# Two products of gate weights beside each of 26 maxima in the lead-in of the attention

## The chip, the cores and the metric

The kernel runs on one core of a Trainium2 chip. The metric is device time in microseconds (us), less is better. The engines are TensorE (PE; its weight loads are PEld), VectorE (DVE), ScalarE (ACT), GpSimd (POOL) and SyncE (SP, which here issues the DMAs). TensorE runs at one of two granted clocks, 2.4 GHz (shown as 1.00) or 1.2 GHz (0.50).

## The reference, cut to what matters

The reference is a macaron block on x of shape (2, 1024, 256): a feed-forward part, causal attention, the feed-forward part again.

```python
x = x + 0.5 * ffn(layernorm(x), w_gate, w_up, w_down)      # silu(gate) * up, 2 of 4 kept, down
x = x + attn(layernorm(x), Wq, bq, Wk, bk, Wv, bv, Wo, bo) # 32 heads of 8, 8 key/value heads, rotary, causal
x = x + 0.5 * ffn(layernorm(x), w_gate, w_up, w_down)
```

Inside the attention: `scores = q k^T / sqrt(8)`, masked above the diagonal, then `softmax(scores) @ v`, then `@ Wo + bo`. The softmax subtracts each row's maximum, and this kernel computes that maximum from the scores themselves.

## The kernel before, in words

The program of each engine is written out by hand and the phases follow one another: feed-forward 1, the projections to q, k and v (`qkv`), attention, feed-forward 2. An engine does its instructions in the order in which they stand; between engines there are semaphores.

The attention goes over 16 groups (2 batches by 8 key/value heads; 4 query heads each). In a group TensorE does three kinds of products:

- **maxima** (`maximum_scores`, written to `att_m_ps`, four banks of PSUM): 48 per group, each 128 queries by up to 512 keys, with the operands' 64 rows in the upper half of the array (`m_lane`, partitions 64 to 127). DVE takes the row maximum of each (L1418 where the causal mask is added, L1421 elsewhere), which frees the bank.
- **scores** (`s_head`, written to `att_s_ps`, three banks): keys by queries, with the operands in the lower half of the array (`s_lane`, partitions 0 to 63). ACT takes the exponential (L1471).
- **values** (`value_unit`, `att_o_ps`, L1370): the exponentials times v, over all 128 rows.

A **turn** (`turn_shift`, L1333) transposes the joined maxima of half a group, so that they can be loaded by DMA as two further rows of q and be subtracted in the scores' product.

The order within a group is the string `ORDER`. Ahead of group 0 there is a **lead-in**, the loop over `first_steps` in `tensor`: maxima 0 to 63 (48 of group 0 and 16 of group 1) with the two turns of group 0 among them, and the first 12 scores. Maxima 0 to 3 stand still earlier, in the projections (`first_scores`). Up to maximum 37 there are only maxima and one turn (it stands ahead of maximum 26); from maximum 38 (`S_FROM`) every second maximum is followed by a score. `banks_free(pe, "s")` waits until DVE has read the last unit of the projections (L817) out of the banks that the scores will use. `wait_bank` lets maximum n wait until DVE has taken the maximum four before it.

`wg[0]` is the high part of the feed-forward's gate weights, in SBUF since feed-forward 1.

Of the kernel before, what the change touches and what calls it, by code (L numbers as in the profile page):

```python
# [1161 lines left out]
        dve.tensor_tensor(rows, self.y_ps[pair % 2][:].rearrange("p t c -> p (t c)"), rows, ALU.add).then_inc(self.y_added, 1)  # L1162


def attention_programs(nc, ctx, group_rows, v, region, s_ps, m_ps, o_ps, output, normed, ident_bf, x, bo_row, T, HD, earlier):

# [4 lines left out]
    q, k, m_loaded = group_rows.q, group_rows.k, group_rows.m_loaded  # L1173
    s_lane, m_lane = group_rows.s_lane, group_rows.m_lane
# [43 lines left out]
    S_BANKS = 3  # L1218
# [14 lines left out]
    def steps(g):  # L1233

        count = dict.fromkeys("smtv", 0)
        for kind in ORDER:
            n = count[kind]
            count[kind] += 1
            if kind == "s":
                n += (g * SU + AHEAD) * QPK  # L1240
                taken = not FIRST_HEADS <= n < GROUPS * SU * QPK
            elif kind == "m":
                n += (g + 1) * MU + FIRST_MAXIMA
                taken = n >= GROUPS * MU
            elif kind == "t":
                n += (g + 1) * QC
                taken = n >= GROUPS * QC
            else:
                n += g * SU
                taken = n < LEAD_IN  # L1250
            if not taken:
                yield kind, n
# [7 lines left out]
    def sb(name, shape, dt):  # L1260
        return region.take(f"att_{name}", shape, dt)
# [14 lines left out]
    bo = sb("bo", [P, x.shape[2]], F32)  # L1276
# [25 lines left out]
    banks_free, v_ready = earlier  # L1302
    WEIGHTS_AT = 2
    FIRST_SCORES = M_BANKS
    S_FROM = 38
    STAGE_AT = LEAD_IN
    assert FIRST_HEADS <= (MU - S_FROM + 1) // 2 + FIRST_TURNS[1]
    PAIR_AFTER = {1: 0, 2: 1, 5: 2, 6: 3}
# [5 lines left out]
    def wait_bank(pe, step):  # L1314
        if step in BANK_USER:
            kind, n = BANK_USER[step]
            pe.wait_ge(m_taken if kind == "m" else shift_t_ready, n + 1)

    def maximum_scores(pe, n):
        g, m = divmod(n, MU)  # L1320
        t, h, kc, cols = M_UNITS[m]
        if m == 0:
            pe.wait_ge(m_loaded[g % 2], 16 * 2 * (g // 2 + 1))
        wait_bank(pe, ("m", n))
        pe.matmul(m_ps[BANK["m", n]][:, :cols], q[g % 2][m_lane, h, t * P:(t + 1) * P],  # L1325
                      k[g % 2][m_lane, kc * N:kc * N + cols],
                  start=True, stop=True).then_inc(m_done, 1)

    def turn_shift(pe, n):
        pe.wait_ge(shift_ready, n + 1)  # L1330
        wait_bank(pe, ("t", n))
        for t in range(TPC):
            last = pe.transpose(t_ps[BANK["t", n]][:, t * P:(t + 1) * P],  # L1333
                                shift[n % QC][:, t, :, :].rearrange("p h s -> p (h s)"), ident_bf[:])
        last.then_inc(t_done, 1)
# [7 lines left out]
    def tensor(pe):  # L1343
        def s_head(n):
            g, u, h = n // (SU * QPK), n // QPK % SU, n % QPK
            qc, pieces = S_UNITS[u]
            if h == 0 and u == 0:
                pe.wait_ge(s_loaded[g % 2], 16 * 2 * (g // 2 + 1))
            if h == 0 and u in CHUNK_FIRST:
                pe.wait_ge(shift_loaded[qc], 16 * QPK * (g + 1))  # L1350
            if n >= S_BANKS:
                pe.wait_ge(exp_done, n - S_BANKS + 1)
            for kb, q0, w, at in pieces:
                last = pe.matmul(s_ps[n % S_BANKS][:, at:at + w], k[g % 2][s_lane, kb * P:(kb + 1) * P],  # L1354
                                 q[g % 2][s_lane, h, qc * N + q0:qc * N + q0 + w], start=True, stop=True)
            last.then_inc(s_done, 1)

        def value_unit(g, u):
            qc, pieces = S_UNITS[u]
            n = g * SU + u  # L1360
            if u == 0:
                pe.wait_ge(v_staged, g + 1)
            if u in CHUNK_FIRST:
                pe.wait_ge(o_taken, QC * g + qc)
            pe.wait_ge(exp_done, QPK * (n + 1))
            if u in DIAGONAL:
                pe.wait_ge(masked, g * sum(map(len, MASKS)) + sum(map(len, MASKS[:u + 1])))
            for kb, q0, w, at in pieces:
                for h in range(QPK):
                    last = pe.matmul(o_ps[32 * h:32 * (h + 1), q0:q0 + w], vs[g % 2][:, kb, :],  # L1370
                                     probs[u % len(probs)][:, h, at:at + w],
                                     start=(u in CHUNK_FIRST), stop=(u in CHUNK_LAST), skip_group_check=True)
            last.then_inc(pv_done, 1)

        def group(g):
            for kind, n in steps(g):
                if kind == "s":
                    s_head(n)
                elif kind == "m":
                    maximum_scores(pe, n)  # L1380
                elif kind == "t":
                    turn_shift(pe, n)
                else:
                    u = n % SU
                    value_unit(g, u)
                    if g == LAST and u in PAIR_AFTER:
                        if PAIR_AFTER[u] == 0:
                            pe.wait_ge(m_taken, GROUPS * MU)
                            pe.wait_ge(shift_t_ready, GROUPS * QC)
                        output.project(pe, PAIR_AFTER[u])  # L1390
                    if g == LAST and u == TURN_AFTER:
                        normed.transpose(pe, 0)

        pe.sem_inc(pv_done, len(probs))
        heads = 0
        for kind, n in first_steps[FIRST_SCORES:]:
            if kind == "t":
                turn_shift(pe, n)
                continue
            maximum_scores(pe, n)  # L1400
            if n >= MU or (n >= S_FROM and (n - S_FROM) % 2 == 0):
                if heads == 0:
                    banks_free(pe, "s")
                if heads < FIRST_HEADS:
                    s_head(heads)
                    heads += 1
        for u in range(LEAD_IN):
            value_unit(0, u)
        for g in range(GROUPS):
            group(g)  # L1410
# [94 lines left out]
    def gpsimd(pool):  # L1505
# [19 lines left out]
        def split_maxima(g, qc):  # L1525

            if qc:
                pool.wait_ge(top_ready, g + 1)
                whole = top[:]
            else:  # L1530
                pool.wait_ge(m_taken, g * MU + MU_HALF)
                whole = maxima[:, :, :TPC, 0].rearrange("p h t -> p t h")
            pool.tensor_copy(shift[qc][:, :, :, 0], whole).then_inc(high_ready, 1)
            pool.wait_ge(high_ready, QC * g + qc + 1)
            pool.tensor_tensor(shift[qc][:, :, :, 1], whole, shift[qc][:, :, :, 0], ALU.subtract)\
                .then_inc(shift_ready, 1)
# [15 lines left out]
        def group(g):  # L1552
            for kind, n in steps(g):
# [4 lines left out]
                elif kind == "m" and n % MU == MU - 1:  # L1558
                    split_maxima(n // MU, 1)
                elif kind == "v" and n % SU == STAGE_AT and g < LAST:  # L1560
                    pool.wait_ge(pv_done, g * SU + len(probs))
# [106 lines left out]
def build(nc, x_in, w_qkv, bias_cols, bv, w_o, bo, w_gate, w_up, w_down, cos_t, sin_t, out, HD=8, SPLIT=4):  # L1668
    B, T, C = x_in.shape
# [6 lines left out]
    with ExitStack() as ctx:  # L1676
# [3 lines left out]
        x = sb("x", [P, TILES, C], F32)  # L1680
        ident = sb("ident", [P, P], F32)
        ident_bf = sb("ident_bf", [P, P], BF16)
        parts = ("hi", "lo")
        wg = [sb(f"wg_{n}", [P, KT, BLKS, J, P], F32R) for n in parts]
# [15 lines left out]
        v = low.take("v", [P, KVH, TILES, HD], F32)  # L1700
        group_rows = GroupRows(nc, ctx, low, q_rows, k_rows, T, HD)
# [30 lines left out]
        for b in range(BLKS):  # L1732
# [11 lines left out]
        qkv, follower, earlier = qkv_programs(nc, ctx, x, normed1, TILES // FIRST, qkv_raw[:], qkv_raw_loaded, bias_cols, bv, cos_t, sin_t,  # L1744
                                              q_rows, k_rows, v, group_rows, qkv_homes, qk_ps, between)
# [7 lines left out]
        normed2 = NormedChunks(nc, ctx, "ffn2", x, ident, N, xt_ps=xt2,  # L1753
                               region=Homes(hole, {"ffn2_xn": m_hole, "ffn2_xt_hi": m_hole, "ffn2_xt_lo": m_hole}))
        late_hole = Region(nc, hole.at)
        att_region = Region(nc, above)
        late = Region(nc, late_at)
        output = Output(nc, ctx, late, hole, x, w_o.rearrange("(k p) n -> p k n", p=P), inverse_rows, KVH, C // HD // KVH, HD, T, N, out_ps)
        attention, before_groups, first_scores, first_maxima, hooks = attention_programs(
            nc, ctx, group_rows, v, att_region, s_ps, m_ps, o_ps, output, normed2, ident_bf, x, bo, T, HD, earlier)  # L1760
        between["fills"] += [lambda pool: group_rows.fill_q(pool, 0),
                    lambda pool: (group_rows.fill_k(pool, 0), before_groups(pool)),
                    lambda pool: (group_rows.fill_q(pool, 1), group_rows.fill_k(pool, 1))]
# [53 lines left out]
```

## Time and profile before

| | us |
|---|---|
| median of 3 runs | 829.38 (826.87 to 832.43) |
| the profiled execution, its own time | 832.21 |
| its span, first to last instruction | 830.7 |
| PE busy | 774.4 (93%) |
| DVE busy | 721.2 (87%) |
| ACT busy | 491.5 (59%) |
| attention's 512 maxima of L1418, on DVE | 234.3 |
| attention's 256 maxima of L1421, on DVE | 175.9 |
| mean granted clock of TensorE | 0.965 |

A row of the timeline is: start, duration, engine, line, operation, what is written and read, the array's rows by columns, the shape, and in brackets how long the engine was idle before it and what ended that. Matmuls are pipelined, so the distance between two starts is what one costs in a series, and not its duration.

### The profile page before, as it was taken

To read this page: it belongs to the slowest core of one execution; us is meant where nothing else is said; L and a number is where in the kernel's file an instruction comes from. 1 tells how busy PE (TensorE), PEld (TensorE's weight loads), DVE (VectorE), ACT (ScalarE), POOL (GpSimd) and SP (SyncE) were. 2 spreads that over 40 slices of the span, in tenths; PEclk is the share of its full clock that TensorE was granted. 3 is DMA by queue.
4 is the path that set the end of the run, shared out by engine and by line. 5 is a ranking of instruction groups with operands and counts; after the bars stand their busy time and mean duration, and the time that the engine had idled before them with its cause. 6 is when DMAs were issued, how large, how long until landed. Compare 5 with 4: busy or idle time off the path is not lost.

```text
span 830.7 us, 15658 instructions
## 1 busy us (share of the span) xinstructions
PE 774.4 (93%) x5168; PEld 508.7 (61%) x5168; DVE 721.2 (87%) x1862; ACT 491.5 (59%) x949; POOL 262.3 (32%) x359
## 2 busy tenths in 40 slices
PE   4999999989899999999999989999899999999996
PEld 3787887977654544444444444444444468888886
DVE  3989999986797999999999989999987259999997
ACT  6444443311135888888888868888678734443441
POOL 1143533058720332322322222155315210534330
PEclk9999999999857999999999989999999999999999
DMA  8100000026913321233311332533313000000001
GB/s 294 53 0 2 0 1 1 1 107 173 297 33 69 71 66 37 61 74 72 70 41 39 72 70 54 132 67 76 72 21 85 15 8 1 1 26 1 26 2 51
DMA packets 21968, 48.62 MB, mean 59 GB/s; under 512 B 3744, under 2 KB 8224, under 8 KB 21376
## 3 DMA queue, kind: packets, MB, share of 16 engines
q1 hardware_dynamic: 21824, 47.56, 21.9%
q8 instruction: 41, 0.67, 0.4%
q14 instruction: 39, 0.32, 0.1%
q10 hardware_dynamic: 64, 0.07, 0.0%
HBM read 19.63 MB, written 14.16 MB: 41 GB/s over the span
## 4 chain that ended last, share of the span: by engine, by line
PE 61%; DVE 20%; issue 8%; POOL 5%; ACT 5%; DMA 1%; PEldq 0%; DVEq 0%; PEld 0%; SPq 0%; ACTq 0%; POOLq 0%
PE att_o_ps L1370 17%; PE att_m_ps L1325 15%; PE att_s_ps L1354 10%; PE ffn_gate L218 5%; PE ffn_up L218 5%; PE ffn_y_ps L351 5%; DVE ffn_hs L524 2%; DVE ffn_h L566 2%; POOL qkv_turned L859 2%; POOL qkv_parts L864 2%; ACT att_probs L1471 2%; DVE att_maxima L1421 2%; DVE att_scratch L1418 1%; DVE ffn_rank L510 1%; DVE ffn_pair_max L498 1%
## 5 line engine op out<-in xcount | busy, mean ns | idle before, releaser
L1471 ACT ACTIVATE att_probs<-att_s_ps 128x512 f32<-128x512 f32 (+1 forms) x640 | 314.3, 558 | 92.4 <-PE att_s_ps L1354 90.4
L1325 PE MATMUL att_m_ps<-k,q 64*128 64x512 f32 (+3 forms) x768 | 240.9, 413 | 15.5 <-DVE att_maxima L1418 13.6
L1418 DVE CUSTOM_DVE_ANT_0 att_scratch<-att_m_ps,att_causal 128x512 bf16<-128x512 f32 (+3 forms) x512 | 234.3, 485 | 20.9 <-PE att_m_ps L1325 17.9
L1354 PE MATMUL att_s_ps<-q,k 64*128 64x512 f32 (+3 forms) x768 | 223.3, 392 | 3.9 <-ACT att_probs L1471 3.9
L1325 PEld LDWEIGHTS att_m_ps<-k,q 64*128 64x128 f32 x768 | 132.9, 196 | 105.2 <-DVE att_maxima L1418 57.4
L1421 DVE TENSOR_REDUCE att_maxima<-att_m_ps 128x1 f32<-128x512 f32 x256 | 175.9, 687 | 11.5 <-PE att_m_ps L1325 11.3
L1370 PE MATMUL att_o_ps<-att_probs,att_vs 128*32 128x512 f32 (+3 forms) x1536 | 161.4, 508 | 1.6 <-POOL att_probs L1510 1.6
L1510 POOL TENSOR_SCALAR_AFFINE_SELECT att_probs<-att_probs 128x512 f32<-128x512 f32 x128 | 79.9, 637 | 262.3 <-ACT att_probs L1471 262.3
L1354 PEld LDWEIGHTS att_s_ps<-q,k 64*128 64x128 f32 x768 | 122.5, 190 | 64.8 <-ACT att_probs L1471 62.0
L630 POOL TENSOR_TENSOR ffn_hs_lo<-ffn_hs,ffn_hs_hi 128x512 fp32r<-128x512 f32 x48 | 76.6, 1621 | 106.4 <-ACT ffn_hs_hi L427 106.4
L454 ACT ACTIVATE ffn_a<-ffn_h 128x512 f32<-128x512 f32 x64 | 40.5, 633 | 106.8 <-DVE ffn_h L566 106.8
L351 PE MATMUL ffn_y_ps<-wd_hi,ffn_hs_hi 128*128 128x256 f32 x256 | 73.8, 288 | 6.2 <-DVE x L554 2.7
L351 PE MATMUL ffn_y_ps<-wd_lo,ffn_hs_hi 128*128 128x256 f32 x256 | 73.0, 285 | 0.0
L351 PE MATMUL ffn_y_ps<-wd_hi,ffn_hs_lo 128*128 128x256 f32 x256 | 72.9, 285 | 0.0
L1370 PEld LDWEIGHTS att_o_ps<-att_probs,att_vs 128*32 128x32 f32 x1536 | 34.1, 110 | 56.4 <-issue 41.8
L566 DVE TENSOR_TENSOR ffn_h<-ffn_up,ffn_silu 128x512 f32<-128x512 f32 x64 | 43.6, 682 | 23.0 <-ACT ffn_silu L449 22.0
L218 PE MATMUL ffn_gate<-ffn_xt_hi,wg_hi 128*128 128x512 f32 x128 | 52.2, 408 | 3.6 <-DVE ffn_h L566 1.6
L351 PEld LDWEIGHTS ffn_y_ps<-wd_hi,ffn_hs_hi 128*128 128x128 f32 x256 | 49.4, 193 | 9.4 <-DVE x L554 2.9
L218 PE MATMUL ffn_gate<-ffn_xt_lo,wg_hi 128*128 128x512 f32 x128 | 50.8, 397 | 0.9 <-DVE ffn_xt_lo L199 0.9
L427 ACT ACTIVATE ffn_hs_hi<-ffn_hs 128x512 fp32r<-128x512 f32 x56 | 35.0, 632 | 27.0 <-DVE ffn_hs L524 27.0
L218 PE MATMUL ffn_gate<-ffn_xt_hi,wg_lo 128*128 128x512 f32 x128 | 50.9, 398 | 0.0
L218 PE MATMUL ffn_up<-ffn_xt_lo,wu_hi 128*128 128x512 f32 x128 | 50.7, 396 | 0.0
(114 smaller groups left out, 1166.8 us busy)
## 6 DMA issues: line engine op xcount, KB each, us to landing
q_rows<-qkv_parts SPq DMA_DIRECT2D x16, 512.0 KB, 4.6
q<-q_rows SPq DMA_DIRECT2D x16, 512.0 KB, 4.6
q<-q SPq DMA_DIRECT2D x16, 512.0 KB, 4.3
k_rows<-qkv_parts SPq DMA_DIRECT2D x8, 256.0 KB, 3.0
k<-k_rows SPq DMA_DIRECT2D x16, 128.0 KB, 5.2
k<-k SPq DMA_DIRECT2D x16, 128.0 KB, 4.3
q<-att_shift_t SPq DMA_DIRECT2D x128, 4.0 KB
out_num<-att_sums SPq DMA_DIRECT2D x128, 16.0 KB
```

Of the source, the lines that this page charges most:

```text
L218: last = pe.matmul(bank, w[w_part], xt[:, k, :], start=(k == 0 and n == 0), stop=(k == self.KT - 1 and n == 2))
L351: last = pe.matmul(y_ps[:, t, :], hp[:, blk, j, rows], wp[:, blk, j, :], start=(blk == 0 and j == 0 and m == 0 and t % 2 == 0), stop=(blk ...
L454: act.activation(a[:, blk, j, :], h[:, blk, j, :], ACT.Abs).then_inc(abs_ready, 1)
L566: dve.tensor_tensor(h[:, blk, j, :], gu[j % 2][1][:], silu[:, j % 2, :], ALU.mult).then_inc(h_ready, 1)
L630: pool.tensor_tensor(hs_lo[:, blk, j, :], hs[:, j, :], hs_hi[:, blk, j, :].bitcast(F32), ALU.subtract).then_inc(lo_ready, 1)
L1325: pe.matmul(m_ps[BANK["m", n]][:, :cols], q[g % 2][m_lane, h, t * P:(t + 1) * P], k[g % 2][m_lane, kc * N:kc * N + cols], start=True, stop ...
L1354: last = pe.matmul(s_ps[n % S_BANKS][:, at:at + w], k[g % 2][s_lane, kb * P:(kb + 1) * P], q[g % 2][s_lane, h, qc * N + q0:qc * N + q0 + w ...
L1370: last = pe.matmul(o_ps[32 * h:32 * (h + 1), q0:q0 + w], vs[g % 2][:, kb, :], probs[u % len(probs)][:, h, at:at + w], start=(u in CHUNK_FI ...
L1418: dve.tensor_tensor_reduce(out=scratch[bank][:, :n], in0=m_ps[bank][:, :n], in1=causal[:, N - n:], scale=1.0, scalar=LOWEST, op0=ALU.add, ...
L1421: dve.tensor_reduce(top_of, m_ps[bank][:, :n], mybir.AxisListType.X, ALU.max).then_inc(m_taken, 1)
L1471: act.activation(probs[u % len(probs)][:, h, SPAN[u]], s_ps[n % S_BANKS][:, SPAN[u]], ACT.Exp, scale=SCALE).then_inc(exp_done, 1)
L1510: pool.affine_select(out=blk, in_=blk, compare_op=ALU.is_ge, fill=0.0, base=0, pattern=[[0, QPK], [1, P]], channel_multiplier=-1).then_inc ...
```

## The change

After each of the maxima 12 to 37, TensorE does two further products (`HOLD = 2`) of 64 rows by 128 columns with 512 moving columns, both operands out of `wg[0]`, with the operands in the lower half of the array. They are written to the three banks `att_s_ps`, which nothing reads until the first score overwrites them. The wait for these banks, which stood ahead of the first score (after maximum 38), stands now also ahead of the first added product. No semaphore is raised by the added products and no other engine's program changes.

```diff
-def attention_programs(nc, ctx, ..., T, HD, earlier):
+def attention_programs(nc, ctx, ..., T, HD, earlier, weights):
...
     S_FROM = 38
+    HOLD_FROM = 12
+    HOLD = 2
...
             maximum_scores(pe, n)
+            if HOLD_FROM <= n < S_FROM:
+
+                if n == HOLD_FROM:
+                    banks_free(pe, "s")
+                for i in range(HOLD):
+                    pe.matmul(s_ps[(HOLD * n + i) % S_BANKS][:], weights[s_lane, 0, 0, i, :],
+                              weights[s_lane, 0, 0].rearrange("p j q -> p (j q)"), start=True, stop=True)
             if n >= MU or (n >= S_FROM and (n - S_FROM) % 2 == 0):
...
-            nc, ctx, group_rows, v, att_region, s_ps, m_ps, o_ps, output, normed2, ident_bf, x, bo, T, HD, earlier)
+            nc, ctx, group_rows, v, att_region, s_ps, m_ps, o_ps, output, normed2, ident_bf, x, bo, T, HD, earlier, wg[0])
```

On TensorE, where maximum 12 stands (the third row from the top; `att_m_ps` are the maxima, `wg_hi` the added products), before:

```order
L1325 MATMUL att_m_ps<-k_52,q_51 128x384 [waits att_m_taken]
L1325 MATMUL att_m_ps<-k_52,q_51 128x256 [waits att_m_taken]
L1325 MATMUL att_m_ps<-k_52,q_51 128x384 [waits att_m_taken]
L1325 MATMUL att_m_ps<-k_52,q_51 128x256 [waits att_m_taken]
L1325 MATMUL att_m_ps<-k_52,q_51 128x384 [waits att_m_taken]
L1325 MATMUL att_m_ps<-k_52,q_51 128x256 [waits att_m_taken]
L1325 MATMUL att_m_ps<-k_52,q_51 128x512 [waits att_m_taken]
```

and now:

```order
L1327 MATMUL att_m_ps<-k_52,q_51 128x384 [waits att_m_taken]
L1327 MATMUL att_m_ps<-k_52,q_51 128x256 [waits att_m_taken]
L1327 MATMUL att_m_ps<-k_52,q_51 128x384 [waits att_m_taken]
L1408 MATMUL att_s_ps<-wg_hi 128x512 [waits qkv_by_ready]
L1408 MATMUL att_s_ps<-wg_hi 128x512
L1327 MATMUL att_m_ps<-k_52,q_51 128x256 [waits att_m_taken]
L1408 MATMUL att_s_ps<-wg_hi 128x512 x2
L1327 MATMUL att_m_ps<-k_52,q_51 128x384 [waits att_m_taken]
L1408 MATMUL att_s_ps<-wg_hi 128x512 x2
```

Two products stand between each maximum and the next; the maxima keep their own waits and their order.

On TensorE, at the end of the stretch (maximum 37, then 38 and the first scores), before:

```order
L1325 MATMUL att_m_ps<-k_52,q_51 128x384 [waits att_m_taken]
L1325 MATMUL att_m_ps<-k_52,q_51 128x512 [waits att_m_taken]
L1354 MATMUL att_s_ps<-q_51,k_52 128x512 [waits att_shift_loaded0,s_loaded0,qkv_by_ready]
L1325 MATMUL att_m_ps<-k_52,q_51 128x384 [waits att_m_taken]
L1325 MATMUL att_m_ps<-k_52,q_51 128x512 [waits att_m_taken]
L1354 MATMUL att_s_ps<-q_51,k_52 128x512
```

and now:

```order
L1327 MATMUL att_m_ps<-k_52,q_51 128x384 [waits att_m_taken]
L1408 MATMUL att_s_ps<-wg_hi 128x512 x2
L1327 MATMUL att_m_ps<-k_52,q_51 128x512 [waits att_m_taken]
L1356 MATMUL att_s_ps<-q_51,k_52 128x512 [waits att_shift_loaded0,s_loaded0,qkv_by_ready]
L1327 MATMUL att_m_ps<-k_52,q_51 128x384 [waits att_m_taken]
L1327 MATMUL att_m_ps<-k_52,q_51 128x512 [waits att_m_taken]
L1356 MATMUL att_s_ps<-q_51,k_52 128x512
```

From maximum 38 on nothing is added and nothing has moved.

## Rows read from the trace of the kernel before

**Rows 1.** The page: share of the chain that ended last.

```profile
PE 61%; DVE 20%; issue 8%; POOL 5%; ACT 5%; DMA 1%; PEldq 0%; DVEq 0%; PEld 0%; SPq 0%; ACTq 0%; POOLq 0%
```

**Rows 2.** Busy time by stretch: stretch, its length, engines' busy us (instructions), PEclk, DMA share, GB/s.

```profile
220.50:223.90 3.40, 1.80 (x8) 1.05 (x6) 3.40 (x15) 0.63 (x1) 2.60 (x3) 1.00 0.96 278
...
224.00:236.00 12.00, 11.49 (x29) 6.81 (x28) 11.17 (x41) 1.22 (x2) 4.95 (x11) 0.50 0.61 192
236.00:246.00 10.00, 9.85 (x35) 5.89 (x34) 9.96 (x30) 6.20 (x12) 1.60 (x4) 0.50 0.00 1
246.00:258.00 12.00, 11.85 (x52) 6.01 (x50) 8.71 (x38) 3.80 (x8) 2.53 (x6) 0.50 0.47 105
258.00:261.40 3.40, 3.40 (x18) 1.82 (x20) 3.05 (x10) 2.53 (x5) 0.00 (x0) 0.50 0.15 30
261.60:280.00 18.40, 17.65 (x152) 8.65 (x145) 16.46 (x56) 14.83 (x32) 3.53 (x8) 1.00 0.07 17
```

**Rows 3.** DVE in the lead-in: last read of the projections, maxima 8, 12, 16, 32 and 38.

```profile
220.51 0.74 DVE L817 SCALAR_TENSOR_TENSOR qkv_by_sin<-qkv_swapped,qkv_biases,qkv_sin 128x512 f32<-128x512 f32 x1
...
222.81 0.55 DVE L1418 CUSTOM_DVE_ANT_0 att_scratch<-att_m_ps,att_causal 128x384 bf16<-128x384 f32 x1
...
224.45 0.55 DVE L1418 CUSTOM_DVE_ANT_0 att_scratch<-att_m_ps,att_causal 128x384 bf16<-128x384 f32 x1
...
226.37 0.69 DVE L1421 TENSOR_REDUCE att_maxima<-att_m_ps 128x1 f32<-128x512 f32 x1 [0.19 <-issue]
226.98 0.28 DVE L1418 CUSTOM_DVE_ANT_0 att_scratch<-att_m_ps,att_causal 128x128 bf16<-128x128 f32 x1
...
231.41 0.69 DVE L1421 TENSOR_REDUCE att_maxima<-att_m_ps 128x1 f32<-128x512 f32 x1 [0.64 <-PE att_m_ps L1325]
...
234.24 0.69 DVE L1421 TENSOR_REDUCE att_maxima<-att_m_ps 128x1 f32<-128x512 f32 x1
...
237.46 0.69 DVE L1421 TENSOR_REDUCE att_maxima<-att_m_ps 128x1 f32<-128x512 f32 x1
```

**Rows 4.** Busy time by stretch, where the clock fell.

```profile
223.00:224.00 1.00, 0.91 (x4) 0.53 (x3) 1.00 (x5) 0.63 (x1) 0.26 (x2) 0.94 1.04 401
```

**Rows 5.** PE at the full clock, both halves of the array in series.

```profile
268.44 0.50 PE L1354 MATMUL att_s_ps<-q,k 64*128 64x512 f32 x1
268.78 0.39 PE L1325 MATMUL att_m_ps<-k,q 64*128 64x512 f32 x1
268.78 0.39 PE L1354 MATMUL att_s_ps<-q,k 64*128 64x512 f32 x1
269.01 0.39 PE L1325 MATMUL att_m_ps<-k,q 64*128 64x512 f32 x1
```

**Rows 6.** PE at the low clock, products of one half in series.

```profile
604.19 0.62 PE L1354 MATMUL att_s_ps<-q,k 64*128 64x512 f32 x1
604.51 0.62 PE L1325 MATMUL att_m_ps<-k,q 64*128 64x512 f32 x1
604.61 0.62 PE L1354 MATMUL att_s_ps<-q,k 64*128 64x512 f32 x1
```

**Rows 7.** Busy time by stretch: three later low stretches and what stood before them.

```profile
483.80:486.60 2.80, 1.78 (x13) 1.12 (x17) 2.80 (x10) 2.35 (x7) 0.99 (x3) 1.00 0.88 227
486.90:490.00 3.10, 3.10 (x20) 1.34 (x16) 2.78 (x8) 1.55 (x4) 0.74 (x2) 0.50 0.49 104
490.20:493.40 3.20, 2.31 (x18) 1.28 (x16) 2.61 (x8) 2.02 (x4) 1.16 (x3) 1.00 0.59 123
...
599.40:606.00 6.60, 5.86 (x32) 3.15 (x32) 5.00 (x16) 2.92 (x7) 0.00 (x0) 0.50 0.31 66
```

**Rows 8.** DVE: the maxima of groups 0, 1, 2 and 3 are joined.

```profile
243.49 0.19 DVE L1436 TENSOR_REDUCE att_top<-att_maxima 128x16 f32<-128x32 f32 x1
...
272.30 0.19 DVE L1436 TENSOR_REDUCE att_top<-att_maxima 128x16 f32<-128x32 f32 x1
...
297.79 0.19 DVE L1436 TENSOR_REDUCE att_top<-att_maxima 128x16 f32<-128x32 f32 x1
...
323.29 0.19 DVE L1436 TENSOR_REDUCE att_top<-att_maxima 128x16 f32<-128x32 f32 x1
```

**Rows 9.** The page: weight loads of the scores.

```profile
L1354 PEld LDWEIGHTS att_s_ps<-q,k 64*128 64x128 f32 x768 | 122.5, 190 | 64.8 <-ACT att_probs L1471 62.0
```

More of the change, by code:

```diff
@@ L1162, in add, with attention_programs @@
         dve.tensor_tensor(rows, self.y_ps[pair % 2][:].rearrange("p t c -> p (t c)"), rows, ALU.add).then_inc(self.y_added, 1)
-def attention_programs(nc, ctx, group_rows, v, region, s_ps, m_ps, o_ps, output, normed, ident_bf, x, bo_row, T, HD, earlier):
+def attention_programs(nc, ctx, group_rows, v, region, s_ps, m_ps, o_ps, output, normed, ident_bf, x, bo_row, T, HD, earlier, weights):
     q, k, m_loaded = group_rows.q, group_rows.k, group_rows.m_loaded
```

## The prediction

> **What bounds the kernel now.** I read the page's chain first. TensorE holds 61% of it and DVE 20% [rows 1], so over the whole kernel TensorE's time counts most. That share says little of the 15 us which the change touches, so I next read busy time by stretch around the lead-in [rows 2]. The reader is to see two things there. First, the granted clock is 1.00 up to 223.9, 0.50 from 224 to 261.4, and 1.00 again from 261.6. Second, from 224 to 236, where there are only maxima and one turn, DVE is busy 11.17 of 12 us, and from 236 to 246 it is busy 9.96 of 10. So DVE is the bound up to 246, low clock or not. Between 246 and 258 DVE has only 8.71 busy of 12, and PE 11.85: there the low clock costs something.
>
> Then I read DVE itself [rows 3]. It takes maximum 12 at 224.45 and maximum 38 at 237.46: 26 maxima in 13.0 us, 0.50 each. It waits noticeably for TensorE only once, 0.64 us ahead of maximum 26, behind the turn. Taken singly, a pair of 512 and 128 columns (maxima 16 to 23) costs 0.61 + 0.20 = 0.81 us (226.37 to 226.98, and 0.28 less its overlap).
>
> What the low clock costs as a whole is read from the joins of the maxima [rows 8]: from group 1's to group 2's it is 297.79 - 272.30 = 25.5 us, and the same from 2 to 3; from group 0's to group 1's it is 28.8. So 3.3 us are lost between 243.5 and 272.3, and that is nearly all behind the place of the added products.
>
> **The change, part by part.** It adds 52 products with their 52 weight loads, on TensorE alone, and moves one wait forward. It removes nothing.
>
> *The wait for the banks.* It now stands ahead of the first added product, behind maximum 12. It ends when DVE has done its last read of the projections, at 220.51 + 0.74 = 221.25. Maximum 12 itself needs DVE to be done with maximum 8, which ends at 222.81 + 0.55 = 223.36 [rows 3]. The wait is over 2.1 us before anyone reaches it: 0 us. If that cover were gone, every later maximum would stand behind it; 2.1 us is a lot of cover.
>
> *Does the clock fall all the same?* The mean 0.94 over 223 to 224 puts the fall at 223.88 [rows 4]. The first added product can't start before 223.4. In the 3.4 us before the fall PE is busy 1.80 us and stands idle the rest, since DVE is the slower one [rows 2], and the change can fill at most the last 0.5 us of that. So what the clock was lowered for is still there, and I expect it to fall at about the same place. An execution in which it falls a little later, or not at all, is possible, since the filled stretch begins right there.
>
> *An added product at either clock.* At the full clock two products of 512 columns on one half of the array start 0.23 us apart, while the other half does the same [rows 5]; at the low clock 0.42 us [rows 6]. Two per maximum make 0.47 and 0.85 us (I take 0.425 for one). The maximum itself runs on the other half meanwhile, as s and m do at 268.78, so it adds nothing. But TensorE works in order: maximum n+1 stands behind two products of maximum n, so the pace of the maxima cannot be better than this.
>
> *At the full clock* 0.47 stands against DVE's 0.405 for maxima 16 to 23 and 0.50 on average: TensorE falls back by 8 x 0.065 = 0.5 us and gets it back in the wider maxima behind. DVE's 0.64 us of waiting behind the turn is what can be had back in the best case, but that turn waits for POOL too. Sum about 0 (0.5 either way).
>
> *At the low clock* 0.85 stands against 0.50 (0.41 for maxima 12 to 23). TensorE becomes the bound, and DVE, banks and all, waits for it. Each maximum that falls into a low stretch costs 0.44 us among the first twelve and 0.35 on average. Nothing covers this: the scores from maximum 38 on, the first exponentials and the second turn all stand behind it in order, and DVE takes group 1's maxima as they come.
>
> *How long would it stay low?* That is the price that rows of before can only bound. One end: it comes back after one of the short low stretches seen later, 3.1 us (486.9 to 490.0) to 6.6 us (599.4 to 606.0), in which both halves of the array were kept at work [rows 7]. The other end: it stays low for all 26, as it did from 224 to 261 with PE busy 9.85 of 10 us in one part [rows 2]; a busy TensorE alone does not bring it back. With the added products one half works all the time and the other some third of it, which lies between these cases. I take the longer of the short stretches, 6.6 us, as the nearest row: 6.6 / 0.85 = 8 maxima, 8 x 0.44 = 3.5 us. Of this 0.5 us is cover (maximum 12's scores were ready, at 223.4 + 0.5, before DVE came at 224.45), and the 0.64 us at the turn is no longer waited for separately: 3.5 - 0.5 - 0.6 = **+2.4 us**.
>
> *What comes back.* The 3.3 us lost behind 243.5 would come back only if the clock were high from 246 to 261. The added products end at maximum 37. Behind them come the same maxima and scores as before, paced by DVE, and at the full clock they leave PE idle much as from 490.2 to 493.4, busy 2.31 of 3.2, where the clock fell again [rows 7]. So even a clock held through the 26 maxima falls in 236 to 246, and the costly part behind is as it was: 0 us.
>
> The sum against the profiled execution is 832.2 + 2.4 = 834.6. That execution is 2.8 us above the median of the runs (829.4), so against the median it is 829.4 + 2.4 = **832** (rounded).
>
> **Rule against row.** Three products of a half start 0.34 and 0.23 us apart, each with its own weight load, whose mean is 190 ns [rows 5, 9]; the load is hidden. The Trainium skill ("TensorE: Matmul & The Clock Gate", section "Part 3: Packing small matmuls — row/col tiling") says that a weight load overlaps running matmuls only where the row groups differ, and both added products use the same. By that rule the sum would be that of the fourth rival below; the trace disagrees with it for products in series.
>
> **The rivals.**
>
> *1. The low clock stays (slower).* The same mechanism, its long end: from two thirds of the 26 maxima on. All of them: 26 x 0.85 = 22.1 us for what takes 13.0, so +9.1 us, 838.5; two thirds (17 of them, 12 at 0.44 and 5 at 0.35, less 1.1) +5.9, 835.3. Against it: rows 7, where the clock came back in 3 to 7 us. For it: rows 2, where it didn't in 34 us with PE just as busy. It is over 1% (8.3 us) only if the clock is not back before about the 24th of the 26.
>
> *2. The clock does not fall before the products begin, and they hold it.* Cost about 0, no gain behind either: 829.4. For it: they start within half a microsecond of the fall. Against it: the idle stretch in front is not changed.
>
> *3. It does what it seems to be for (faster).* The clock is high through the lead-in and also behind, to 261. The 3.3 us of the joins and up to 0.9 us of DVE's waits come back: 829.4 - 3.3 = 826.1, at best 825.2. Against it: the ten microseconds without added products.
>
> *4. Every product pays its weight load.* 0.23 + 0.19 = 0.42 us at the full clock too, so 0.85 per maximum for all 26: +9, 838.5. Rows 5 speak against it.
>
> **How the numbers follow.** Chances: the forecast (clock falls, back within the first dozen or so; +1 to +4) 0.38; rival 1 0.28, of which 0.10 for over 1%; rival 2 0.17; rival 3 0.13; rival 4 0.04, of which 0.02 for over 1%. A change of under 1% (8.3 us) can't be told from none by this measurement, the runs before alone spread over 5.6 us. Slower by over 1% has 0.10 + 0.02 = 0.12; faster by over 1% needs twice what rival 3 gives, 0.02; within 1% the rest, 0.86. The range: from 826, which leaves out the better half of rival 3 (0.07), to 837, which takes in rival 1 up to +7.6 and leaves out its end and rival 4 (0.13).
>
> **What would show it.** In the profile after: the clock falls near 224 with the first added products in front of it, and is 0.50 for some 3 to 10 us. In the low part maxima of L1327 start 0.85 us apart and DVE is idle ahead of each, waiting for PE; in the high part 0.47 to 0.6. DVE's join of group 0 moves from 243.5 to about 246. From about 240 to 262 the clock is 0.50 again and the distance of the joins of groups 0 and 1 stays near 28.8. What would make it wrong: a join of group 0 at 243 to 244 (rival 2), 249 to 253 (rival 1 or 4, told apart by the clock), or a distance of 25.5 between the joins (rival 3).

## The result and the profile after

The changed kernel is slower by 0.7%: 837.5 us median (830.2 to 843.3, 20 runs) against 830.4 (826.3 to 840.0, 20 runs) for the kernel before, ratio 1.0073, 95% interval 1.0052 to 1.0094. The ratio leaves out executions over 1.5% above the fastest of their kernel, the medians do not; by the ratio it is 6.1 us, by the medians 7.1. Two later comparisons gave 1.0077 (1.0051 to 1.0104) and 1.0094 (1.0065 to 1.0123). That is within the 1% which I had called no change, but clear of noise. I had forecast +2.4 us.

The profiled execution took 833.9 us (span 832.4), 1.7 more than the profiled one before, and the page looks alike:

```profile
PE 63%; DVE 20%; issue 7%; ACT 5%; POOL 4%; DMA 1%; PEldq 0%; DVEq 0%; PEld 0%; SPq 0%; ACTq 0%; POOLq 0%
...
L1430 DVE TENSOR_REDUCE att_maxima<-att_m_ps 128x1 f32<-128x512 f32 x256 | 175.9, 687 | 11.0 <-PE att_m_ps L1327 10.9
```

Busy time by stretch (length; PE, PEld, DVE, ACT, POOL busy us; PEclk; DMA share; GB/s), to be read against [rows 2]:

```profile
221.50:224.80 3.30, 1.70 (x10) 1.09 (x9) 3.30 (x15) 0.63 (x1) 2.53 (x3) 1.00 1.02 282
225.00:228.00 3.00, 3.00 (x14) 2.54 (x12) 2.28 (x12) 0.63 (x1) 2.28 (x2) 0.50 1.05 400
228.50:240.00 11.50, 11.34 (x72) 8.73 (x70) 10.86 (x34) 1.67 (x2) 2.17 (x9) 1.00 0.30 76
...
242.00:246.00 4.00, 3.98 (x12) 2.12 (x13) 3.96 (x11) 1.75 (x5) 0.15 (x1) 0.50 0.00 0
246.00:258.50 12.50, 12.22 (x53) 6.76 (x53) 9.82 (x42) 4.16 (x8) 3.98 (x10) 0.50 0.36 87
```

The clock still falls, right behind the half-empty stretch (PE busy 1.70 of 3.3 us), with the first added products at 224.4. Here it is back by 228.5. From 242 on it is low again, up to 265.8. On DVE the low part looks like this:

```profile
227.13 0.42 DVE L1427 CUSTOM_DVE_ANT_0 att_scratch<-att_m_ps,att_causal 128x256 bf16<-128x256 f32 x1 [0.29 <-PE att_m_ps L1327]
...
228.31 0.69 DVE L1430 TENSOR_REDUCE att_maxima<-att_m_ps 128x1 f32<-128x512 f32 x1 [0.74 <-PE att_m_ps L1327]
```

DVE now waits for TensorE ahead of maxima 15 and 16; in the kernel before it did so, up to maximum 38, only at the turn [rows 3]. At the turn it still waits, 0.61 us. And TensorE itself, first at the low and then at the full clock:

```profile
226.31 1.05 PE L1408 MATMUL att_s_ps<-wg_hi 64*128 64x512 f32 x2
226.74 0.47 PE L1327 MATMUL att_m_ps<-k,q 64*128 64x128 f32 x1
227.16 1.05 PE L1408 MATMUL att_s_ps<-wg_hi 64*128 64x512 f32 x2
...
229.51 0.61 PE L1408 MATMUL att_s_ps<-wg_hi 64*128 64x512 f32 x2
229.90 0.50 PE L1327 MATMUL att_m_ps<-k,q 64*128 64x512 f32 x1
229.97 0.61 PE L1408 MATMUL att_s_ps<-wg_hi 64*128 64x512 f32 x2
```

A pair of added products starts every 0.85 us (227.16 - 226.31) and then every 0.46 (229.97 - 229.51). The joins, to be read against [rows 8]:

```profile
245.60 0.19 DVE L1445 TENSOR_REDUCE att_top<-att_maxima 128x16 f32<-128x32 f32 x1
...
275.04 0.19 DVE L1445 TENSOR_REDUCE att_top<-att_maxima 128x16 f32<-128x32 f32 x1
...
300.53 0.19 DVE L1445 TENSOR_REDUCE att_top<-att_maxima 128x16 f32<-128x32 f32 x1
```

Executions reach the lead-in at slightly different times. To compare traces I measure from DVE's last read of the projections (L817), which starts at 220.51 in the kernel before and at 221.48 here. From there to group 0's join it is 22.98 us before and 24.12 here, +1.1.

What this one trace does not show is the median's 7 us. Each run lists its mean granted clock, and the time goes with it: of the changed kernel's runs those at 0.977 to 0.979 took 830 to 834 us, those at 0.971 to 0.973 took 835 to 837, those at 0.963 took 841 to 843. But at the same mean clock of 0.967 the kernel before takes 830 to 834 us and the changed one 837 to 840. So the mean clock alone does not explain the 7 us: either the low clock costs more in the changed kernel, because of where it falls, or the added products cost their time whatever the clock is.

### The profile page after: what moved, and what is told of

It reads as the page before. It is cut to its first block, busy times and chain, and to the rows that moved or that the text cites. A ratio compares the mean times of both kernels' runs of the same rounds, so it can differ in the third digit from the quotient of the medians.

```text
span 832.4 us, 15762 instructions
## 1 busy us (share of the span) xinstructions
PE 772.8 (93%) x5220; PEld 512.3 (62%) x5220; DVE 724.5 (87%) x1862; ACT 492.0 (59%) x949; POOL 262.2 (32%) x359
## 4 chain that ended last, share of the span: by engine, by line
PE 63%; DVE 20%; issue 7%; ACT 5%; POOL 4%; DMA 1%; PEldq 0%; DVEq 0%; PEld 0%; SPq 0%; ACTq 0%; POOLq 0%
PE att_o_ps L1372 17%; PE att_m_ps L1327 15%; PE att_s_ps L1356 10%; PE ffn_gate L218 6%; PE ffn_up L218 5%; PE ffn_y_ps L351 4%; DVE ffn_hs L524 3%; DVE ffn_h L566 2%; ACT att_probs L1480 2%; DVE att_scratch L1427 1%; PE out_y_ps L1152 1%; DVE att_maxima L1430 1%; DVE ffn_pair_min L499 1%; POOL qkv_turned L859 1%; PE att_s_ps L1408 1%
## 5 line engine op out<-in xcount | busy, mean ns | idle before, releaser
L1327 PE MATMUL att_m_ps<-k,q 64*128 64x512 f32 (+3 forms) x768 | 237.6, 405 | 15.4 <-DVE att_maxima L1427 12.8
L1356 PE MATMUL att_s_ps<-q,k 64*128 64x512 f32 (+3 forms) x768 | 220.6, 389 | 4.2 <-ACT att_probs L1480 4.0
L1327 PEld LDWEIGHTS att_m_ps<-k,q 64*128 64x128 f32 x768 | 129.8, 191 | 101.3 <-DVE att_maxima L1427 58.4
L351 PEld LDWEIGHTS ffn_y_ps<-wd_hi,ffn_hs_hi 128*128 128x128 f32 x256 | 49.4, 193 | 10.2 <-DVE x L554 2.9
L351 PEld LDWEIGHTS ffn_y_ps<-wd_lo,ffn_hs_hi 128*128 128x128 f32 x256 | 49.6, 194 | 1.5
L218 PE MATMUL ffn_up<-ffn_xt_hi,wu_hi 128*128 128x512 f32 x128 | 50.5, 394 | 0.0
```

What stands on the lines that cost most here:

```text
L218: last = pe.matmul(bank, w[w_part], xt[:, k, :], start=(k == 0 and n == 0), stop=(k == self.KT - 1 and n == 2))
L351: last = pe.matmul(y_ps[:, t, :], hp[:, blk, j, rows], wp[:, blk, j, :], start=(blk == 0 and j == 0 and m == 0 and t % 2 == 0), stop=(blk ...
```

## The experiments

Theory 1: what costs is low clock within the 26 maxima, where TensorE becomes the bound; how long it lasts differs between executions. Theory 2 (the rival): the added products cost their time at any clock. What the added products write is read by nobody, in the change and in all kernels below.

**The changed kernel again.**

> The changed kernel once more, for further executions and one more trace. Theory 1 (the price is the time at the low clock within the 26 maxima, and differs from one execution to the next): 830 to 843 us, median near 837, and over the executions the time rises as the mean granted clock falls; the trace's join of group 0 lies at 245.6 if the clock is back after about 3.4 us, at up to 252 if it stays low. Theory 2 (the added products cost the same at either clock): the join of group 0 lies at the same place whatever the clock did.

837.3 us median of 9 runs. This trace is of the other kind:

```profile
218.50:222.00 3.50, 2.22 (x10) 1.38 (x10) 3.11 (x11) 0.63 (x1) 2.76 (x3) 1.00 0.87 203
222.10:239.00 16.90, 16.87 (x63) 12.62 (x63) 10.81 (x39) 1.85 (x3) 5.97 (x12) 0.50 0.54 169
239.20:245.80 6.60, 6.24 (x36) 4.27 (x33) 6.51 (x19) 2.35 (x4) 0.00 (x0) 1.00 0.00 1
246.00:266.00 20.00, 19.70 (x80) 10.96 (x78) 16.33 (x63) 8.66 (x18) 4.15 (x10) 0.50 0.30 68
```

```profile
249.87 0.19 DVE L1445 TENSOR_REDUCE att_top<-att_maxima 128x16 f32<-128x32 f32 x1
```

The clock is low for 17 us, TensorE is busy all of it and DVE only 10.8. DVE waits for TensorE ahead of most maxima there, the longest ahead of maximum 26, behind the turn:

```profile
230.61 0.69 DVE L1430 TENSOR_REDUCE att_maxima<-att_m_ps 128x1 f32<-128x512 f32 x1 [0.51 <-PE att_m_ps L1327]
...
236.96 0.69 DVE L1430 TENSOR_REDUCE att_maxima<-att_m_ps 128x1 f32<-128x512 f32 x1 [1.61 <-PE att_m_ps L1327]
```

L817 starts at 220.35, so the join comes after 29.5 us, 6.5 more than before. It is the same program as the one with +1.1. Theory 2 can't explain that.

**And a third time.**

> The changed kernel a third time: 837 us median; its trace should again have the join of group 0 at 243 + 0.35 to 0.44 us for each maximum that falls into the low clock, whatever length the low stretch has.

838.8 us median of 12 runs; in the trace the clock is low from 222.6 to 239.4 again (PE busy 16.7 of 16.8 us, DVE 10.2), join after 30.0 us, +7.0. By the working of the prediction 17 us at 0.85 are 20 maxima, 12 x 0.44 + 8 x 0.35 - 1.1 = 7.0; the two measured 6.5 and 7.0. The sum fits better than its terms do, as the section on the prediction shows.

The two profiled executions took 835.4 and 834.4 us, only 3.2 and 2.2 more than the profiled one before. Some of the loss is made up by join 1 (+5.9 and +5.8). The rest is that the profiled execution before lost time later on, in the low stretches of [rows 7]: its joins 9 and 10 are 30.4 us apart and its joins 13 and 14 31.0, against 27.9 and 29.3 in the third trace, which has no low stretch there.

**One product in place of two.**

```diff
-    HOLD = 2
+    HOLD = 1
```

> One added product per maximum in place of two. Theory 1: at the low clock one costs 0.43 us, less than the 0.50 us that DVE takes per maximum, so TensorE never becomes the bound: join of group 0 within 1 us of the kernel before, 830.5 us median, ratio 1.000 to 1.002. Theory 2 (each added product costs its own time): half the loss, 834.

831.4 us median (12 runs) against 831.3, ratio 1.0008 (0.9983 to 1.0033). The execution profiled was the longest of the 12, 842.1 us. Its trace has the low clock in the same place, and for twice as long as the first trace of the change:

```profile
221.30:224.50 3.20, 1.60 (x8) 0.89 (x6) 3.20 (x13) 0.59 (x2) 2.50 (x2) 1.00 0.98 271
224.70:231.40 6.70, 6.70 (x32) 3.87 (x30) 6.52 (x26) 0.63 (x1) 5.19 (x11) 0.50 0.98 320
```

But DVE is busy 6.52 of 6.7 us there, and the join comes after 22.7 us, 0.3 sooner than before. One product of 0.42 us per maximum hides behind DVE's 0.50, even at the low clock. Theory 2 wanted 3.5 us. What made this execution long lies behind the last join, where the clock is low for 17 us, in a part that the change does not touch:

```profile
650.00:664.00 14.00, 14.00 (x66) 8.68 (x58) 0.69 (x1) 4.73 (x9) 1.92 (x3) 0.50 0.05 9
```

From the join of group 15 to the last instruction it takes 198.6 us, and 190.4 in the kernel before, which has the full clock there.

**384 columns in place of 512.**

```diff
-                    pe.matmul(s_ps[(HOLD * n + i) % S_BANKS][:], weights[s_lane, 0, 0, i, :],
-                              weights[s_lane, 0, 0].rearrange("p j q -> p (j q)"), start=True, stop=True)
+                    pe.matmul(s_ps[(HOLD * n + i) % S_BANKS][:, :384], weights[s_lane, 0, 0, i, :],
+                              weights[s_lane, 0, 0].rearrange("p j q -> p (j q)")[:, :384], start=True, stop=True)
```

> Two products as in the change, with 384 moving columns in place of 512. Theory 1: 0.64 us per maximum at the low clock, +0.14 against DVE's 0.50, so the long low case costs 26 x 0.14 less the 1.1 us of cover, some 2.5 us in place of 8: 832 to 833, ratio 1.002 to 1.004. Rival (time follows the columns at any clock): three quarters of the loss, 835.5.

833.5 us median (12 runs) against 830.8, ratio 1.0058 (1.0024 to 1.0092). The median lies between the two theories' numbers (832 to 833, and 835.5), and the interval holds both; the ratio itself is that of theory 2 (1.0057), the median is nearer to theory 1. Its trace had a short low stretch (226.6 to 230.0) and no loss up to the join, so this run doesn't decide.

**Three products.**

```diff
-    HOLD = 2
+    HOLD = 3
```

> Three products per maximum from 12 to 37 in place of two. Theory 1: 0.70 us per maximum at the full clock and 1.28 at the low, against DVE's 0.50: +5 us where the clock is high, up to +20 where it is low; 840 to 851 us, above the change by 3 to 14. Rival (52 products cost 7 us at any clock): 78 cost 10.5, 841.

851.7 us median (850.7 to 856.2, 5 runs), ratio 1.025 (1.020 to 1.031): 21 us more than the kernel before, where the rival allowed 10.5 for 78 products; and 14 more than the change for 26 further products, where it allowed 3.5. In the trace the clock is low from 226.8 to 260.7:

```profile
226.80:260.70 33.90, 33.90 (x113) 25.88 (x111) 14.93 (x45) 1.22 (x2) 5.16 (x11) 0.50 0.24 71
```

```profile
229.03 1.48 PE L1408 MATMUL att_s_ps<-wg_hi 64*128 64x512 f32 x3
229.89 0.79 PE L1327 MATMUL att_m_ps<-k,q 64*128 64x512 f32 x1
230.31 1.48 PE L1408 MATMUL att_s_ps<-wg_hi 64*128 64x512 f32 x3
```

The maxima come every 1.28 us. The join stands 43.4 us behind L817's start, +20.4; the working gives 26 x 1.28 - 13.0 - 1.1 = 19.2. And TensorE busy every microsecond did not bring the clock back for 34 us.

**The stretch in front filled.**

```diff
-    HOLD_FROM = 12
+    HOLD_FROM = 7
```

> The same two products, but from maximum 7 on, so that the idle stretch in front of maximum 12 is filled. Theory 1: the clock does not fall near 224 and stays high up to about 240; no maximum is paced at 0.85 us; join of group 0 at 243 to 244.5, then the clock falls among the scores as before; 830 us, ratio 0.998 to 1.003. Theory 2: five more maxima with products, so 1 us slower than the change, 838.

830.5 us median (12 runs), ratio 1.0004 (0.9973 to 1.0036), with ten products more than the change. The trace:

```profile
221.00:224.40 3.40, 3.25 (x21) 2.60 (x22) 3.40 (x18) 0.63 (x1) 2.66 (x3) 1.00 1.02 305
224.60:241.40 16.80, 15.98 (x91) 11.33 (x89) 16.02 (x52) 5.06 (x8) 4.28 (x11) 1.00 0.40 117
241.60:262.00 20.40, 20.10 (x93) 10.98 (x94) 15.91 (x62) 8.74 (x17) 4.14 (x10) 0.50 0.29 67
```

With TensorE busy 3.25 of 3.4 us in the place where it had been busy 1.7, the clock does not fall, and the join comes after 22.8 us: two products per maximum are free at the full clock, which theory 2 excludes. It also shows the other half of the forecast. The clock was held through all 26 maxima and fell at 241.5, in the part without added products; joins 0 and 1 are 29.2 us apart (243.18 and 272.38), and nothing is gained.

**Products through the whole lead-in.** Here all of them go into `o_ps`, two behind each maximum from 7 to 37 and one behind each from 38 on, but for 48 to 54.

```diff
-            if HOLD_FROM <= n < S_FROM:
+            if HOLD_FROM <= n:
...
-                for i in range(HOLD):
-                    pe.matmul(s_ps[(HOLD * n + i) % S_BANKS][:], weights[s_lane, 0, 0, i, :],
+                for i in range(HOLD if n < S_FROM else 0 if MU <= n < MU + 7 else 1):
+                    pe.matmul(o_ps[:], weights[s_lane, 0, 0, i, :],
```

> Two products from maximum 7 to 37, then one behind each of the maxima 38 to 47 and 55 to 63, all into the bank of the values, which is free in the lead-in. Theory 1: the clock stays high from the projections through the scores of the lead-in into group 0; the joins of groups 0 and 1 stand 25.5 to 26.5 us apart in place of 28.8, and the kernel takes about 827 us, ratio 0.996. Theory 2: 83 products in place of 52, so 840 or more.

832.1 us median (12 runs), ratio 1.0022 (0.9991 to 1.0053): not faster. In its trace the clock fell at 223.9 in spite of the filling from 7 on, and was low for 17 us. There are still 0.67 us without work ahead of the first product, but so there are in from_7, where it did not fall: over 3.4 us around this pause TensorE is busy 2.73 us in both. So this start can come out either way. Join 0 stands at 251.8, 30.5 us behind L817, +7.5. Behind it, with the clock mostly high, the joins are 25.9 us apart (251.79 and 277.67) in place of 28.8. Both effects, the loss in front and the gain behind, stand in one trace.

**From maximum 4 on.**

> Products from maximum 4 on, directly behind the projections, into the first scores' bank, which is free one unit of the projections earlier; two each up to maximum 37, then one behind each of the maxima 38 to 47 and 55 to 63 in the values' bank. Theory 1: TensorE has no idle stretch left in which the clock falls, so it stays high from the projections into group 0; joins of groups 0 and 1 at 243.5 to 245 and 25.5 to 26.5 us apart; 827 to 828 us, below the kernel before by 2 to 4, with few executions above 832. Rival (every added product costs time at any clock): 90 products, over 840.

Its diff adds to the last one the start at maximum 4, the first scores' bank for the products up to maximum 37, and a wait ahead of them that ends one read of the projections earlier. 831.2 us (12 runs), ratio 1.000 (0.997 to 1.003). The start worked (PE busy 17.1 of 17.4 us from 224.0 to 241.4 at the full clock, join after 22.8 us), the hole at 48 to 54 did not:

```profile
241.60:244.80 3.20, 2.48 (x14) 1.07 (x11) 3.16 (x10) 1.59 (x5) 0.34 (x2) 1.00 0.03 5
245.00:265.00 20.00, 19.78 (x97) 11.68 (x98) 13.65 (x57) 7.61 (x15) 3.58 (x8) 0.50 0.29 68
```

Behind the hole the clock is low, and the products that still follow are then paid for: the joins are 30.5 us apart, 1.7 more than in the kernel before.

**From maximum 4 on, one product each from 12 on.**

> As from_4, but one product in place of two for the maxima 12 to 37. Theory 1: where the clock falls all the same TensorE is not the bound (0.43 us per maximum at the low clock), so no execution pays for it; but at the high clock TensorE does less and the clock may fall more often than with two. 827 to 830 us. Rival: less than from_4 by 26 products' cost.

831.2 us (12 runs), ratio 1.0017 (0.9981 to 1.0053). With one product TensorE is busy 2.20 of 3.2 us from 229.7 to 232.9, and the clock falls there; in the 3.4 us of low clock that follow it costs nothing (join after 23.1 us). The same hole as in from_4 follows.

**The hole filled too.**

```diff
-                for i in range(HOLD if n < S_FROM else 0 if MU <= n < MU + 7 else 1):
+                for i in range(HOLD if n < S_FROM else 1):
```

> As from_4, but the hole at maxima 48 to 54, in front of which the clock fell at 244.9 there, is filled too, with one product each. Theory 1: at the full clock this costs 7 x 0.07 = 0.5 us (two products of one half in 0.47 us against DVE's 0.40), and the clock stays high into group 0: joins of groups 0 and 1 at 244.5 and 25.5 to 26.5 us apart, 828 us, ratio 0.996 to 0.998. Rival (something else than the clock makes the first groups 28.8 us long): the distance stays over 28, 831 to 832.

```profile
224.00:240.00 16.00, 15.80 (x104) 12.53 (x102) 15.20 (x54) 4.09 (x7) 5.21 (x11) 1.00 0.53 160
240.00:246.00 6.00, 5.51 (x31) 3.21 (x32) 5.96 (x21) 3.43 (x8) 1.61 (x4) 1.00 0.01 3
246.00:258.00 12.00, 11.37 (x84) 5.89 (x84) 11.24 (x46) 6.36 (x13) 2.53 (x6) 1.00 0.47 107
```

```profile
244.04 0.19 DVE L1449 TENSOR_REDUCE att_top<-att_maxima 128x16 f32<-128x32 f32 x1
...
268.80 0.19 DVE L1449 TENSOR_REDUCE att_top<-att_maxima 128x16 f32<-128x32 f32 x1
```

In the trace this does all that was wanted: the full clock from the projections into group 0, the first join where it was (22.8 us) and the second 24.8 us behind it, 4.0 less than in the kernel before. That execution took 826.0 us. Yet the 12 runs lie between 826.0 and 834.7, median 830.2 against 831.4, ratio 0.9999 (0.9970 to 1.0029).

**That kernel again.**

> no_hole once more, since its executions lie between 826 and 835 and one trace shows only the short end. Theory 1: in the long executions the clock falls somewhere in the lead-in after all and the two products of each maximum are paid for there (join of group 0 well above 244), or it falls in the feed-forward parts; a trace of such an execution shows which. Rival: a long execution with the clock high throughout the lead-in and the joins at their places. 828 to 832 us median.

831.0 us (12 runs), ratio 0.9986 (0.9953 to 1.0018). The second trace, of 830.3 us, has the same lead-in (full clock, joins 24.8 us apart) and low stretches elsewhere, about 189 to 197 in the projections and 490 to 494 and 596 to 603 in the attention. No trace fell on an execution of 833 us or more.

The mean clocks of the executions say more. One minus the mean clock, doubled and times the span, is the time at the low clock. For the 107 executions of the kernel before that stand beside the experiments its median is 51 us, of which the lead-in and what follows it hold 37 in the profiled one, so some 14 lie elsewhere. For the 24 executions of no_hole it is 26 us, and in both traces none of it lies between the projections and join 1. In either kernel an execution takes about 0.37 us longer for each microsecond at the low clock (least squares over those executions). So my estimate is 12 us more of low clock elsewhere, 4.4 us, which is what the lead-in gave back (4.2 up to join 1). That these 12 us lie outside the lead-in in the long executions too, and why the clock falls there more often, no trace shows.

**Two products each at the end.**

> As no_hole, with two products behind each of the maxima 55 to 63. Theory 1: 9 x 0.07 us more at the full clock, and fewer executions in which the clock falls before the first values; 828 to 829 us. Rival: as for no_hole, and 9 products more.

830.1 us (12 runs), ratio 1.0006 (0.9969 to 1.0043), joins 26.3 us apart: no better than no_hole.

From the start of L817, in the profiled executions:

| | to join 0 | to join 1 | low clock in the 26 maxima |
|---|---|---|---|
| before | 22.98 | 51.79 | 13 us and on |
| the change, first trace | 24.12 | 53.56 | 3 us |
| the change, second and third | 29.52, 30.01 | 57.66, 57.56 | 17 us |
| one product | 22.71 | 51.56 | 7 us |
| 384 columns | 22.59 | 51.49 | 3 us |
| three products | 43.39 | 72.12 | 34 us |
| from 7 | 22.82 | 52.02 | none |
| whole lead-in | 30.46 | 56.34 | 17 us |
| from 4 | 22.83 | 53.37 | none |
| from 4, one from 12 on | 23.07 | 53.61 | 3 us |
| no_hole, both traces | 22.84, 22.87 | 47.60, 47.63 | none |
| two at the end | 22.82 | 49.13 | none |

## Why the prediction was right and where it was wrong

*The wait for the banks: right.* It costs nothing. In from_7 it stands five maxima earlier and TensorE does stand idle for it (0.67 us), and still the join has not moved.

*The clock falls all the same: right*, in all three traces of the change, between 222 and 225. That the half-empty stretch in front is what it falls for was argued, and the kernels that fill it bear it out. With products from maximum 4 on, the clock did not fall there in any of five traces; from 7 on, with 0.67 us left empty, it fell in one of two. From 12 on it fell in six of six (one, two and three products, and 384 columns), and in the kernel before.

*The price at either clock: right.* 0.85 us per maximum at the low clock and 0.46 at the full one were measured as forecast, and one product (free) and three (+20.4 against 19.2) follow the same working.

*What was added and taken off around it: three terms were off, and they nearly cancel.* First, DVE's 0.41 us per maximum holds for 16 to 23. Maxima 12 to 23 take 5.29 us in the kernel before, 0.44 each, so the price among them is 0.41 and not 0.44, and for the 14 behind them (7.72 us) it is 0.30 and not 0.35. Second, I took off 0.6 us for the wait at the turn. It did not go: 0.61 us in the first trace, 1.61 in the second and third. Third, a low stretch of 17 us doesn't hold 20 maxima. In the second trace the clock falls at 222.0, 1.3 us ahead of the first added product, and the turn stands within the stretch; DVE takes maxima 12 to 28 in it, which are 17 (19 in the third trace, where the clock falls 0.2 us ahead of that product). The 6.5 us of that trace are +4.4 from maximum 12 to 24, +1.3 from 24 to 26, over the turn, and +0.8 behind. That 20 maxima gave 7.0 is in part luck.

*How long it stays low: wrong, and this is the term that missed.* I took 6.6 us, the longest of the short low stretches of [rows 7], for +2.4 us. The traces show 3 us once (+1.1 to the join) and 17 us twice (+6.5 and +7.0). The medians of all three series lie 6.0 to 7.5 us up, where the 17 us put them, so most executions seem to do what my own rival 1 has for two thirds of the maxima (+5.9); traces there are of three. I had given it 0.28 and the short stretch 0.38. Why it is 3 us in one execution and 17 in another stays open. The rows that were nearest were not the late short stretches, in which values over the whole array stood beside scores and maxima, but the 37 us of [rows 2] (224 to 261.4; I wrote 34), in which TensorE had been busy on half or two halves of the array without getting its clock back. One trace of the changed kernel could also have misled: it shows the short case.

*Nothing comes back behind: right.* Held through 26 maxima the clock fell in the scores behind them (from_7), and the joins stayed 29 us apart. With products there too, 4.0 us came back between the joins in both traces of no_hole, a little more than the 3.3 I had read off the joins; its median did not follow.

*The weight load: right.* Pairs of products on the same half start every 0.46 us with their loads, 0.23 each. (The rows of [rows 5] hold one pair of each half, 0.34 and 0.23 us apart, and not three products of one half; the change has the long series.) By the rule quoted from the Trainium skill ("TensorE: Matmul & The Clock Gate", section "Part 3: Packing small matmuls — row/col tiling") it would have been 0.42 each, an estimate with the 0.19 us of a load; no trace here shows that.

*The range and the sign.* 826 to 837 was for a median of 829.4 before. The measured 837.5 is just past its upper end as a number, and 835.4 with the ratio 1.0073 on 829.4. I forecast no change to be told within 1%; what there is, is slower, by less than that. The result lies inside the range because the range took in most of rival 1, not because of the forecast of +2.4: the ratio makes it 6.1.

## What to carry to other kernels

Work added to hold TensorE's clock must be cheap at the low clock too, since it may meet it, as it did in all three traces of the change: here one product per maximum hid behind VectorE at either clock, and two hid at the full one alone. It has to begin in front of the idle stretch for which the clock falls, and to reach up to the part that needs the clock; a hole at either end undoes it. Even then the whole need not gain: no_hole gave back 4 us in the lead-in and its median did not move. And where the clock differs between executions, one trace shows one case: read the times and mean clocks of many runs beside it before you settle what a change costs.

## What the runs showed of the hardware

- TensorE busy in every microsecond did not bring the full clock back: 33.9 of 33.9 us in the trace with three products, 16.87 of 16.9 in the changed kernel's second.
- The clock fell in the lead-in with no pause of TensorE over 1.3 us in front. In stretches that ended where it fell TensorE was busy 1.70 of 3.3 us, 2.22 of 3.5, 2.20 of 3.2 and 2.48 of 3.2.
- The same program's time goes with the mean granted clock of the execution, over 13 us from the shortest to the longest run; in the kernel before too (826 us at 0.975, 841 at 0.955).
- What low clock costs depends on where it falls: 37 us of it cost about 4 us in the lead-in (before against no_hole), 17 us behind the last join about 8 (the trace with one product), and one stretch of 3.4 us between joins 9 and 10 1.2 us (29.1 against 27.9 us; first and third trace of the change).
